# Seven edits from the last token block to the last normalized tile of a two-layer routed feed-forward kernel

## The reference

```python
x = x + L0_ffn(L0_cond(x))   # cond: a picked 32x32 matrix mixes the rows of each sequence
                             # ffn: softmax router, group-limited top 2 of 16 experts,
                             #   y += gate_e * ((silu(x@w1_e+b1) * (x@w2_e+b2)) @ w3_e + b3), plus a shared expert
x = x + L1_ffn(L1_cond(x))   # cond: every row h is convolved causally with a kernel made from dt, C, A; masked by length
# L1_ffn(t):
h      = relu(t @ up_w) ** 2                       # 512 -> 1024
shared = h @ down_w                                # 1024 -> 512
latent = (t @ fc1_w) @ expert_w                    # 512 -> 256 -> 256
routed = (latent * sum(top2(t @ gate_w))) @ fc2_w  # 256 -> 512
out    = layernorm(shared + routed) * ln_gamma + ln_beta
```

## Time and profile before

| | us |
|---|---|
| median of three runs | 347.64 (346.77 to 349.14) |
| the profiled execution, its own time | 347.7 |
| span of its trace | 345.7 |
| PE busy | 321.8 (93% of the span) |
| DVE, ACT, POOL busy | 187.4, 115.1, 108.4 |

### The profile page before, as it was taken

The page is one execution under the profiler, slowest core; times in us unless marked ns, Lnnn a source line. Parts: engine busy times, 40 slices in busy tenths (PEclk is TensorE's granted clock), DMA queues, the critical chain, the costliest instruction groups (busy, mean ns, idle before and its releaser), DMA issues.

```text
span 345.7 us, 5496 instructions
## 1 busy us (share of the span) xinstructions
PE 321.8 (93%) x1945; PEld 243.8 (71%) x1945; DVE 187.4 (54%) x375; ACT 115.1 (33%) x198; POOL 108.4 (31%) x131
## 2 busy tenths in 40 slices
PE   7699899999999899999997997999998999999992
PEld 2367688988887688886864443578887787888871
DVE  4637896889366233454594378346212356433266
ACT  2462312233832232541045633732213333212210
POOL 8350002547477776643200000998000000000000
PEclk9699999999999999999999899999999999999998
DMA  6999900697677789999688990000000000100002
GB/s 194 365 394 404 379 27 0 199 322 225 186 242 219 219 299 327 335 350 409 240 313 344 332 350 6 3 0 0 2 0 0 3 0 30 63 30 2 0 16 105
DMA packets 32830, 59.93 MB, mean 173 GB/s; under 512 B 7213, under 2 KB 8081, under 8 KB 32804
## 3 DMA queue, kind: packets, MB, share of 16 engines
q1 hardware_dynamic: 25764, 48.95, 40.4%
q0 software_dynamic: 4992, 8.42, 7.0%
q10 hardware_dynamic: 2048, 2.21, 1.8%
HBM read 55.02 MB, written 12.40 MB: 195 GB/s over the span
## 4 chain that ended last, share of the span: by engine, by line
PE 71%; DVE 9%; DMA 9%; issue 4%; POOL 2%; ACT 2%; SPq 1%; ACTq 0%; DVEq 0%; POOLq 0%
PE bank L1561 13%; PE bank L417 12%; PE bank L419 12%; PE bank L418 12%; PE bank L1531 6%; DMA toep<-kpad 4%; PE bank L1525 3%; PE bank L1632 2%; DMA sdt<-in_L_cond_log_dt 2%; PE bank L1407 2%; DMA yg<-ytok 2%; DVE acc L1232 2%; DMA xg<-xrow,tokx 1%; PE bank L1468 1%; PE bank L1439 1%
## 5 line engine op out<-in xcount | busy, mean ns | idle before, releaser
L1561 PE MATMUL bank<-xt,ew 128*128 128x128 f32 x496 | 60.7, 276 | 0.0
L1561 PEld LDWEIGHTS bank<-xt,ew 128*128 128x128 f32 x496 | 58.0, 192 | 0.7 <-issue 0.5
L622 POOL DMA_INDIRECT xg<-xrow,tokx x31 | 33.2, 1070 | 43.5 <-DVE tokx L1052 31.1
L629 POOL DMA_INDIRECT ytok<-yout,dstx x31 | 31.8, 1027 | 27.0 <-DVE yout L1164 19.4
L1316 DVE TENSOR_TENSOR sq<-rel 128x512 f32<-128x512 f32 x16 | 13.3, 834 | 43.4 <-ACT rel L863 43.4
L1531 PE MATMUL bank<-ew,bhid 128*128 128x512 f32 x62 | 31.6, 595 | 0.0
L775 ACT ACTIVATE xt<-bank 128x512 f32<-128x512 f32 x31 | 18.4, 597 | 33.5 <-PE bank L1525 33.4
L417 PE MATMUL bank<-dnh,sqh 128*128 128x512 f32 x64 | 25.2, 393 | 1.7 <-DVE sql L1324 1.6
L1525 PEld LDWEIGHTS bank<-ident,xg 128*128 128x128 f32 x124 | 15.1, 141 | 16.5 <-issue 12.7
L669 POOL TENSOR_TENSOR dnl<-dnraw,dnh 128x512 fp32r<-128x512 f32 x8 | 10.5, 1356 | 48.9 <-ACT dnh L830 48.9
L417 PE MATMUL bank<-ah,uph 128*128 128x512 f32 x64 | 25.1, 393 | 0.0
(11 more groups left out here) (315 smaller groups left out, 611.3 us busy)
## 6 DMA issues: line engine op xcount, KB each, us to landing
ew<-in_L_ffn_ew SPq DMA_DIRECT2D x51, 256.0 KB, 3.7
ew<-in_L_ffn_ew SPq DMA_DIRECT2D x21, 512.0 KB, 10.6
toep<-kpad SPq DMA_DIRECT2D x4, 1536.0 KB, 12.7
yg<-ytok SPq DMA_DIRECT2D x8, 512.0 KB, 3.9
acc<-in_x SPq DMA_DIRECT2D x4, 512.0 KB, 7.4
xrow<-xstage ACTq DMA_DIRECT2D x4, 512.0 KB, 6.8
upraw<-in_L_ffn_up_w SPq DMA_DIRECT2D x1, 2048.0 KB, 10.1
dnraw<-in_L_ffn_down_w SPq DMA_DIRECT2D x1, 2048.0 KB, 16.4
```

The lines of the kernel that those rows point to most:

```text
L622: pool.indirect_dma_start(xg[:, n % XGS, :], None, xrow, bass.IndirectOffsetOnAxis(ap=tokx[:, n:n + 1].bitcast(U32), axis=0), bounds_check ...
L629: pool.indirect_dma_start(ytok, bass.IndirectOffsetOnAxis(ap=dstx[:, n:n + 1].bitcast(U32), axis=0), yout[:, n % YOS, :], None, bounds_che ...
L1561: mm = pe.matmul(bank[2 + n % 2][:, w * P:(w + 1) * P], ew[:, ring(n), col + k * P:col + (k + 1) * P], xt[:, n % 2, k, :], start=(k == 0), ...
```

## The change

1. **Last block.** For n = NB - 1 = 30, `block_y(28)` stands ahead of the hidden products of block 30.
2. **Eight row slots.** `yg` becomes `yg_lo` (four slots where `yg` lay) and `yg_hi` (four in the space of the up weights' rounded part). All eight loads are issued with no wait between them, so the up weights and the fourth Toeplitz piece are issued behind them at once.
3. **Toeplitz rows first.** SP issues the rows of heads 24 to 31 (wait for two groups of the convolution) ahead of the down weights.
4. **Split copy.** ACT copies the last tile into `u_t` in two halves. The convolution starts on the first, and waits for the second at k = 2.
5. **Latent weights.** One half of the product on line 1652 goes ahead of `conv_turn(7)`, one behind it.
6. **Scales.** The spread moves from the latent product of v = 6 to the end of v = 4, and ACT's copies from v = 6 to v = 5.
7. **End of a half.** The down tiles of slice 6 leave the loop. Behind the wait for `lath` and `latl` come two of them (AHEAD_TILES), and then for each tile: the missing down tile of slice 6, the routed product, and the down tile of slice 7, which now signals `rt_done`. `halves_free` puts the matching waits on ACT and DVE.

```diff
+        def rows_of(i):
+            return yg_lo[:, i, :, :] if i < YS else yg_hi[:, i - YS, :, :]
+        def rows_in(i):
+            return (yg_in[i], 16) if i < YS else (st_in[i - YS], (96, 96, 48, 96)[i - YS] + 16)
+        def halves_free(eng, q, j):
+            wait(eng, rt_done, q * TH)
+            if j > 1:
+                wait(eng, dn_done, (q * (JC - 1) + j - 1) * TH)
...
         for i in range(NT):
-            wait(sp, comb_ok, K * (i - YS + 1))
-            sp.dma_start(yg[:, i % YS, :, :], ytok[i * P * K:(i + 1) * P * K, :].rearrange("(p k) t -> p k t", k=K))\
-                .then_inc(yg_in[i % YS], 16)
+            sp.dma_start(rows_of(i), ytok[i * P * K:(i + 1) * P * K, :].rearrange("(p k) t -> p k t", k=K))\
+                .then_inc(rows_in(i)[0], 16)
...
+        sp.wait_ge(conv_done, (C - TS) // 4)
+        toeplitz(0, TS, C - TS, TS // TP)
         sp.wait_ge(comb_ok, K * NT)
         sp.dma_start(dnraw[:, :, :], down_w.rearrange("(j p) n -> p j n", p=P)).then_inc(dn_in, 16)
-        sp.wait_ge(conv_done, (C - TS) // 4)
-        toeplitz(0, TS, C - TS, TS // TP)
...
+        act.wait_ge(xt_done, NT)
+        copy_u(NT - 1, 0, KC // 2)
+        copy_u(NT - 1, KC // 2, KC)
...
-                if v == JC - 2:
+                if v == 5:
                     act.wait_ge(rscb_done, 1)
...
-                wait(dve, dn_done, (v - 1) * TH)
+                halves_free(dve, q, j)
...
+            if n == NB - 1:
+                block_y(n - 2)
             for w, col in enumerate((W1, W2)):
...
-            if n >= 2:
+            if 2 <= n < NB - 1:
                 block_y(n - 2)
...
             for k in range(KC):
+                if k == KC // 2:
+                    pe.wait_ge(u_ok, NT + 1)
...
+        pe.wait_ge(y_added, NT)
+        latent_weights(0)
+        conv_turn(NCG - 1)
+        latent_weights(1)
...
-                   lambda k: (dnh[:, j, :], dnl[:, j, :]), 1, start=(j == 0), stop=False).then_inc(dn_done, 1)
+                   lambda k: (dnh[:, j, :], dnl[:, j, :]), 1, start=(j == 0), stop=(j == JC - 1))\
+                .then_inc(dn_done if j < JC - 1 else rt_done, 1)
...
-                if j:
+                if 0 < j < JC - 1:
                     if v == 1:
                         pe.wait_ge(top_ok, 1)
                     for i in range(TH):
                         down_tile(v - 1, i)
+                if v == 4:
+                    scales_spread()
                 if j == JC - 2:
                     latent(q)
             pe.wait_ge(lath_ok, LC * (q + 1))
             pe.wait_ge(latl_ok, LC * (q + 1))
+            for i in range(AHEAD_TILES):
+                down_tile(q * JC + JC - 2, i)
             for i in range(TH):
-                down_tile(q * JC + JC - 1, i)
+                if i >= AHEAD_TILES:
+                    down_tile(q * JC + JC - 2, i)
                 s = slice(i * P, (i + 1) * P)
                 split3(pe, bank[i][:, :], lambda a: (lath[:, a, s], latl[:, a, s]),
-                       lambda a: (m2h[:, a, :], m2l[:, a, :]), LC, start=False).then_inc(rt_done, 1)
+                       lambda a: (m2h[:, a, :], m2l[:, a, :]), LC, start=False, stop=False)
+                down_tile(q * JC + JC - 1, i)
```

More of the change, by code:

```diff
@@ L75, in adaln_ffn_program @@
     YS = 4
+    AHEAD_TILES = 2
     HOLD = 3
@@ L234, in adaln_ffn_program @@
     r = [raw_at + KC * INT1 * 4]
-    yg = at(r, "yg", [P, YS, K, T])
+    yg_lo = at(r, "yg_lo", [P, YS, K, T])
+    r = [exp_at]
+    yg_hi = at(r, "yg_hi", [P, NT - YS, K, T])
     r = [raw_at]
@@ L809, in _, with copy_u @@
                 act.activation(hidh[:, 2 * q:2 * q + 2, :], hid[:, 2 * q:2 * q + 2, :], ACT.Copy).then_inc(hidh_ok, 1)
-        for i in range(NT):
+        def copy_u(i, k0, k1):
+            act.activation(u_t[:, :, k0:k1, BT * i:BT * i + BT].rearrange("p h k b -> p k b h"),
+                           bank[YBANK[i]][:, k0 * P:k1 * P].rearrange("p (k b h) -> p k b h", k=k1 - k0, b=BT), ACT.Copy)\
+                .then_inc(u_ok, 1)
+        for i in range(NT - 1):
             act.wait_ge(xt_done, i + 1)
-            act.activation(u_t[:, :, :, BT * i:BT * i + BT].rearrange("p h k b -> p k b h"),
-                           bank[YBANK[i]][:, :].rearrange("p (k b h) -> p k b h", k=KC, b=BT), ACT.Copy).then_inc(u_ok, 1)
+            copy_u(i, 0, KC)
+        act.wait_ge(xt_done, NT)
+        copy_u(NT - 1, 0, KC // 2)
+        copy_u(NT - 1, KC // 2, KC)
         act.wait_ge(up_in, 16)
@@ L864, in _ @@
                 act.wait_ge(sq_ok, v + 1)
-                wait(act, dn_done, (v - 1) * TH)
+                halves_free(act, q, j)
                 act.activation(sqh[:, v % 2, :], sq[:, v % 2, :], ACT.Copy).then_inc(sqh_ok, 1)
@@ L1647, in _, with latent_weights @@
                 conv_turn(g - 1)
-        conv_turn(NCG - 1)
-        pe.wait_ge(y_added, NT)
-        for a in range(LC):
+        def latent_weights(a):
             for m in range(LC):
@@ L1676, in down_tile, with scales_spread @@
             split3(pe, bank[i][:, :], lambda k: (sqh[:, v % 2, s], sql[:, v % 2, s]),
-                   lambda k: (dnh[:, j, :], dnl[:, j, :]), 1, start=(j == 0), stop=False).then_inc(dn_done, 1)
+                   lambda k: (dnh[:, j, :], dnl[:, j, :]), 1, start=(j == 0), stop=(j == JC - 1))\
+                .then_inc(dn_done if j < JC - 1 else rt_done, 1)
+        def scales_spread():
+            pe.wait_ge(m2l_ok, LC)
+            pe.wait_ge(rsc_ok, 1)
+            for i in range(NT):
+                mm = pe.matmul(bank[6 + i // TH][:, i % TH * P:(i % TH + 1) * P],
+                               rsc[:, i:i + 1].broadcast_to([P, P]), ident[:, :], start=True, stop=True)
+            mm.then_inc(rscb_done, 1)
         def latent(q):
@@ L1685, in latent @@
             wait(pe, latf_ok, q * LC)
-            if q == 0:
-                pe.wait_ge(rsc_ok, 1)
-                for i in range(NT):
-                    mm = pe.matmul(bank[6 + i // TH][:, i % TH * P:(i % TH + 1) * P],
-                                   rsc[:, i:i + 1].broadcast_to([P, P]), ident[:, :], start=True, stop=True)
-                mm.then_inc(rscb_done, 1)
-                pe.wait_ge(rscb_ok, 2)
+            pe.wait_ge(rscb_ok, 2)
             for a in range(LC):
```

4 lines of the change are left out of this document (2 added, 2 removed).

## The result

| | before | changed |
|---|---|---|
| median, us (14 executions of each) | 347.75 (345.83 to 349.68) | 344.02 (342.75 to 348.72) |
| ratio | | 0.9901, 95% interval 0.9872 to 0.9931 |
| the profiled execution, us | 347.7 | 345.68 |
| span of its trace, mean granted clock | 345.7, 0.981 | 343.8, 0.984 |

The changed kernel is 3.4 us faster by the ratio (1.3% to 0.7%). The two profiled executions are only 2.0 us apart.

The account below looks back on a forecast made before the run. PE, busy 93% of the span, was taken as the bound, through its gaps and slow clock. From 347.7 us the terms summed to -2.2, so 345.5; one clock fall of 1.5 gave 347.0, range 344.3 to 349.4.

Parts of the forecast that it names:

- PE's wait for `latl`: Ahead of slice 6's down tiles in each half: PE stands 2.9 us in place of 0.8.
- The clock stays up at the start of the convolution: First two convolution groups: shorter gaps before them keep the clock at full rate, gain 1.5 us.
- falls at both ends: Rival: the clock falls behind both waits for `latl`, giving 348.5 us, 0.9 above the median; chance 0.25.
- one fall: The forecast case: the clock falls behind one of the two `latl` gaps, costing 1.5 us, 347.0 us; chance 0.34.
- The end of the halves: New order of the last down tiles: costs 2.1 us in the first half and 0.75 in the second.
- the restart: End of the first half: PE starts 0.33 us after `latl` ends at 273.97, so at 274.3.
- The scales: Spread and copies moved earlier: PE's 1.2 us wait for `rscb` at v = 6 goes, gain 1.1 us.
- The slots: Row additions: with eight slots DVE's wait for the last tile's rows goes, gain 1.02 us.
- The block's order: Last block: block 28's copy slips behind `bhid(30)`, costing 0.55 us at the start of the additions.
- none: Case without a fall of the clock at the ends of the halves: 345.5 us; chance 0.22.
- The tiles: Rival: at each half's end six matmuls (1.4 us) run ahead of the wait, covering half the gap, 342.8 us; chance 0.05.
- a front half that gives less: Rival: clock falls at the convolution's start or rows land late, +1.0 to 1.5 us; 348.5 with one fall; chance 0.1.

Follow-up runs that it names:

- r1: Changed kernel with two down tiles of slice 6 ahead of the wait for `lath` and `latl`: 339.58 us, ratio 0.9785 to the kernel before.
- r3: Changed kernel with DVE making `latl` of slice 7 ahead of its `sq`, PE's list unchanged: 336.48 us, ratio 0.9706 to the kernel before.
- r10: Changed kernel with DVE copying y(28) out ahead of `bhid(30)`: 344.2 us, ratio 0.9892 to the kernel before.
- r6: Changed kernel with the down weights ahead of the last Toeplitz rows again: 346.49 us, ratio 0.9964 to the kernel before.
- r8: Changed kernel with the last tile's copy to `u_t` as one operation again: 344.01 us, ratio 0.9892 to the kernel before.
- r9: Changed kernel with both halves of the latent weights behind the last turn again: 343.01 us, ratio 0.9868 to the kernel before.
- r5: Changed kernel with row loads 4 to 7 waiting again for additions of four tiles before: 344.83 us, ratio 0.9911 to the kernel before.
- r0: The changed kernel run again with no edit: 341.76 us, ratio 0.9842 to the kernel before.
- r4: Changed kernel with `block_y(28)` back behind the last hidden products: 344.54 us, ratio 0.9926 to the kernel before.
- r7: Changed kernel with the scales' spread and ACT's copies at v = 6 again: 344.33 us, ratio 0.9913 to the kernel before.

## Why the prediction was right or wrong

**Right: the mechanisms and their places.** PE's wait for `latl` ahead of the down tiles is what ends each half (r1 to r3), 2.67 us long where 2.9 was worked out. `yout` is late behind `bhid(30)` (r10). The Toeplitz rows give 1.6 us (r6), the split copy 0.42 (r8; predicted 0.4), and the latent weights 0 (r9), because PE waits for `al` instead (1.46 us; predicted 1 to 2). The clock stays up at the start of the convolution: the two groups took 1.69 us less, predicted 1.5. The first up product came 4.27 us earlier, predicted 4.0. That the clock held there by the shorter gaps rests on one trace of the kernel before, in which it fell, against thirteen in which it didn't; no run gives both gaps back.

**The sign and the size.** Faster was forecast, by 0.7 us, and 3.4 were measured. The sign was not sure: with falls at both ends the same sum gave 0.9 us slower. The terms below explain 1.3 of the 3.0 us between forecast and median. The other 1.7 are the distance from the profiled execution to the median, and the prediction had no term for them: it was reckoned against one execution of the kernel before.

**Mis-sized terms.** The forecast for an execution with one fall was 347.0, and the profiled one, with one fall, took 345.68. Of the 1.3 us, 0.23 come before the change begins. The end of the halves cost 1.8 and 0.5 us without falls, not 2.1 and 0.75. The step that failed there is the restart: I let PE start 0.33 us behind the end of `latl`, taken from its start behind `sql` in the trace of before, and it started 0.1 behind. The scales gave 1.44, not 1.1: the sum took PE's named wait alone, and 0.2 to 0.3 us around it stand in no row of waits. The slots and the copy together gave 1.53 to the start of the convolution (predicted 1.42), but the parts are less certain. With one copy (r8), 14.70 against 15.82 before leaves 1.1 for the slots; r5 says 0.5. The difference is how late the last tile's rows landed in that execution. The block's order cost 0.66, predicted 0.55, through PE; in the first profile the loads added 0.15.

**The chances of a fall.** I gave each gap six or seven chances in ten, for both alike. Nine traces have the ends of the changed kernel, counting the first and those of r0 and r4 to r10. In them the clock fell behind the first gap seven times and behind the second twice. The price is 1.3 to 1.6 us at either place, predicted 1.5. So in the traces "one fall" was the likeliest case (five of nine), and "none" and "both" (two each) came about as often as given. But three of r0's six executions have no fall at all. That both gaps are alike is not what the traces show: the first fell about as often as given, the second much more rarely, though nine traces are few. What the median got beyond the forecast is the terms above and executions without the slow stretch at the start: r0's, with one fall and without that stretch, took 344.02, the median of the result. The executions of the kernel before vary in the same way (343.82 to 350.08 us beside r0, mean clock 0.979 to 0.996), which is why the ratio, and not the single profile, carries the result. Whether they gain from fast starts as often as those of the changed kernel isn't shown; if not, part of the 3.4 us is luck.

**The rivals.** The tiles did not cover half the gap (5 in 100, 342.8): the order had them behind the wait, and r1, which puts them ahead of it, shows what that would have given, 1.3 us an end. Neither two falls nor a front half that gives less came in the profile.

On the copy the estimate from the Trainium skill (VectorE: DVE Perf Modes, "The TRN2 errata — SBUF-src ops pay a fixed extra latency per instruction") was a gain of 0.21 us. Measured are 0.42: the whole copy takes 1.02 us (r8), and the first half 0.60 in the changed kernel; the second starts 0.41 behind the first and overlaps its end, so the two take 1.07 together. Worked out from 1.02 and 0.60, a copy costs 0.17 us fixed and 1.67 ns for each element. The fixed part is near the Trainium skill's 172 cycles (0.14 us at 1.2 GHz); the time for each element is twice its 0.83 ns. ACT's `rel`, as large but written without a stride, takes 0.60 us, near the 0.57 of the Trainium skill's formula. That the stride makes the difference is likely by this, but wasn't tried alone.

## What to carry to other kernels

An engine that has to feed a wait ought to do that work first when its inputs are old: `latl` stood behind `sq`, which needed the newest product. The order of two lines on DVE was worth 5.3 us by the medians (4.7 by the ratios), nearly as much as all seven edits in the same series (5.5 by r0's ratio). But much of it is repair. In the first profile the edits ahead of the ends gained 5.5 us (the rows of the table from the first addition to the last `rel`, less the 0.8 of the block's order), and the new end of a half gave 3.75 of them back, 1.4 of that by a fall of the clock. When a wait is moved ahead of work that used to cover it, look at what the releasing engine has in its list ahead of the release. When a median can't show an effect of half a microsecond, a distance between two fixed operations in a trace can, to 0.05 us.

## What was unexpected in the hardware

Two gaps of the same length (2.67 us), with the same work on PE before and behind them, were followed by a fall of the clock in 7 of 9 traces at one place and in 2 of 9 at the other. What tells them apart isn't shown. At the start of the convolution the clock held in all thirteen traces with eight slots or half copies, also with either one undone (r5, r8), while in the one trace with neither it fell; which of the two was needed there remains open. At the start of an execution, a wait of 2.0 to 3.0 us for the same transfer was followed by a fall in six traces and by none in three (r3, r4, r7), and in five PE came so late that it didn't wait; everything behind moved by up to 3.6 us with that. In those five the 16 small products from 5.2 us on took 3.64 us in place of 1.92, though the granted clock in the rows is 1.00 there too.
